# An attention and feed-forward kernel: the copy of each finished PV quad out of PSUM moves from VectorE to ScalarE, and the order of work is laid out again for all engines

## What is computed

```python
x = x + layernorm(attention(layernorm(x)))
x = x + layernorm(ffn(layernorm(x)))

# attention: 16 heads of 16 features
q = x @ Wq;  latent = (x @ Wk + x @ Wv) @ W_down_kv
k = latent @ W_up_k;  v = latent @ W_up_v
scores = (q_h @ k_h.T) / 16 * decay[i, j]        # decay = exp(-0.0001 * |i - j|)
out = softmax(scores) @ v_h;  return concat(out) @ Wo

# ffn
xh = x @ hadamard
xq = per-row 4-bit quantization of xh;  wq = ternary quantization of the weight
return xq @ wq.T
```

## Time and profile before

| | |
|---|---|
| median of 3 runs | 1435.21 us (1431.94 to 1436.89) |
| the profiled execution | 1435.05 us, span 1433.2 us, mean granted TensorE clock 0.983 |
| busy, share of the span: PE, DVE, ACT, POOL | 94%, 82%, 77%, 58% |
| ScalarE's exp of off-diagonal units (L909) | 768 instructions, 759.8 us |
| PV matmuls (L720) | 4096 in the page's count, 525.4 us |
| VectorE's copy out of heads_ps (L1150) | 128 instructions, 87.2 us |

### The profile page before, as it was taken

One profiled execution on the slowest core, in us unless ns is written; L12 is line 12 of the kernel. 1 busy time (PEld: TensorE's weight loads), 2 busy tenths in 40 slices (PEclk: granted clock), 3 DMA queues, 4 the chain that ended last, 5 costly groups with the idle time before them and its releaser, 6 DMA issues.

```text
span 1433.2 us, 35971 instructions
## 1 busy us (share of the span) xinstructions
PE 1349.5 (94%) x12330; PEld 600.5 (42%) x12330; DVE 1179.9 (82%) x2739; ACT 1098.2 (77%) x1125; POOL 834.7 (58%) x1238
## 2 busy tenths in 40 slices
PE   5889999999999999999999999999999999999863
PEld 3334444444444444444444444444444444443332
DVE  7567888888888888888888888888888888888655
ACT  1878787888888788878878887887888787787831
POOL 4223655666565666556557655656765655675446
PEclk9999999999999999999999999999999999999986
DMA  6455456556555645656564565655556555555420
GB/s 194 154 167 170 154 172 202 155 164 206 164 182 173 197 156 166 206 157 190 173 190 157 173 201 157 193 175 187 156 177 194 163 185 184 176 156 175 128 77 31
DMA packets 174557, 241.45 MB, mean 168 GB/s; under 512 B 28336, under 2 KB 145200, under 8 KB 174512
## 3 DMA queue, kind: packets, MB, share of 16 engines
q1 hardware_dynamic: 140176, 206.78, 46.5%
q10 hardware_dynamic: 34336, 34.08, 7.7%
HBM read 154.80 MB, written 69.21 MB: 156 GB/s over the span
## 4 chain that ended last, share of the span: by engine, by line
PE 76%; DVE 8%; issue 5%; ACT 4%; DMA 3%; SPq 2%; POOL 2%; DVEq 0%; ACTq 0%; POOLq 0%
PE heads_ps L720 27%; PE scores_ps L707 16%; PE misc_ps L603 8%; PE misc_ps L635 7%; PE misc_ps L660 4%; PE misc_ps L614 3%; PE misc_ps L587 3%; ACT probs L909 2%; DVE x_hl L1204 2%; PE misc_ps L595 2%; PE misc_ps L678 2%; DVE diagonal L1253 2%; DVE weighted L1161 2%; PE misc_ps L625 2%; PE misc_ps L669 1%
## 5 line engine op out<-in xcount | busy, mean ns | idle before, releaser
L909 ACT ACTIVATE probs<-scores_ps 128x1024 f32<-128x1024 f32 x768 | 759.8, 1026 | 248.0 <-PE scores_ps L707 247.9
L720 PE MATMUL heads_ps<-probs,v_sb 128*32 128x512 f32 x4096 | 525.4, 603 | 3.6 <-DVE heads L1150 1.9
L1253 DVE TENSOR_TENSOR diagonal<-scores_ps,comp 128x1024 f32<-128x1024 f32 x256 | 312.2, 1219 | 70.1 <-PE scores_ps L707 70.1
L707 PE MATMUL scores_ps<-q_rep,k_rep 64*128 64x128 f16 (+2 forms) x5120 | 324.6, 251 | 16.0 <-DVE diagonal L1253 9.2
L707 PEld LDWEIGHTS scores_ps<-q_rep,k_rep 64*128 64x128 f16 x5120 | 165.6, 94 | 348.7 <-DVE diagonal L1253 149.5
L916 ACT ACTIVATE probs<-diagonal 128x2048 f32<-128x2048 f32 x128 | 246.0, 1922 | 0.0
L996 POOL TENSOR_TENSOR ln_neg_mean<-zero,ln_moments 128x4 f32<-128x4 f32 (+1 forms) x131 | 34.6, 264 | 356.5 <-DVE ln_moments L1115 356.3
L1161 DVE SCALAR_TENSOR_TENSOR weighted<-misc_ps,edges 128x384 f32<-128x384 f32 x256 | 129.4, 547 | 64.3 <-PE misc_ps L603 33.8
L720 PEld LDWEIGHTS heads_ps<-probs,v_sb 128*32 128x32 f32 x4096 | 91.5, 108 | 171.7 <-issue 169.8
L1038 POOL TENSOR_TENSOR q_hl<-weighted,q_hl 128x768 f16<-128x768 f32 x64 | 105.5, 1648 | 77.5 <-DVE q_hl L1168 77.5
L1043 POOL TENSOR_TENSOR heads_c<-heads_c,den_spread 128x1024 f32<-128x1024 f32 (+1 forms) x33 | 75.7, 2296 | 111.0 <-DMA den_spread<-den_scratch 111.0
(11 more groups left out here) (132 smaller groups left out, 1511.5 us busy)
## 6 DMA issues: line engine op xcount, KB each, us to landing
q_rep<-q_scratch SPq DMA_DIRECT2D x128, 384.0 KB, 4.3
k_rep<-k_scratch SPq DMA_DIRECT2D x256, 192.0 KB, 3.9
q_scratch<-q_hl SPq DMA_DIRECT2D x64, 384.0 KB, 2.6
k_scratch<-k_hl SPq DMA_DIRECT2D x64, 384.0 KB, 3.1
x_in<-in_L_attn_x_dram ACTq DMA_DIRECT2D x32, 512.0 KB, 4.9
heads_c<-heads SPq DMA_DIRECT2D x256, 64.0 KB, 2.5
...
den_spread<-den_scratch SPq DMA_DIRECT2D x256, 64.0 KB, 2.3
```

Of the source, the lines that this page charges most:

```text
L707: ins = mm(scores_ps[:, place + par, at:at + n * P], k_rep[rows, pair, kv_, k_cols], q_rep[rows, pair, qv_, q_cols], start=True, stop=True)
L720: ins = mm(heads_ps[W32 * g:W32 * (g + 1), :], v_sb[:, b.slot, kt, at:at + W32], probs[:, quad % 2, g, kt, :], start=(kt == 0), stop=(kt = ...
L909: nc.scalar.activation(flat[:, :, at:at + S], scores_ps[:, place:place + 2, :], ACT.Exp, scale=EXP_SCALE).then_inc(off_probs, 1)
L1253: v.tensor_tensor(diagonal[:, quad % 2, 2 * two:2 * two + 2, :], scores_ps[:, place:place + 2, :], comp[:].rearrange("p t n -> p (t n)").u ...
```

## The change

The copy of heads_ps becomes an ACTIVATE Copy on ScalarE, with the same waits and the same semaphore; its VectorE instruction is gone. All step lists and closing lists are replaced.

```diff
 TENSOR_STEPS = {
-    1: [("z", 0, 0), ("z", 1, 0), ("pv_end", 3, 0)], 3: [("xT", 0, 0), ("pv_end", 3, 1)], 5: [("xT", 1, 0), ("pv_end", 3, 2)],
-    7: [("pv_end", 3, 3), ("lat", 0, 0)], 9: [("q", 0, 0), ("q", 0, 1)], 11: [("pv", 0, 0), ("x1T", 0, 0)],
-    13: [("x1T", 1, 0), ("pv", 0, 1)], 15: [("k", 0, 0), ("pv", 0, 2), ("k", 1, 0), ("pv", 0, 3)], 17: [("v", 0, 0), ("xh", 0, 0)],
-    19: [("xh", 1, 0), ("pv", 1, 0)], 21: [("pv", 1, 1), ("pv", 1, 2)], 23: [("q", 1, 0), ("q", 1, 1), ("pv", 1, 3)],
-    25: [("y", 0, 0), ("y", 0, 1)], 27: [("pv", 2, 0), ("qintT", 0, 0)], 29: [("y", 1, 0), ("y", 1, 1)],
-    31: [("pv", 2, 1), ("pv", 2, 2), ("pv", 2, 3)],
+    0: [("z", 0, 0), ("z", 1, 0)], 1: [("xT", 0, 0)], 2: [("pv_end", 3, 0), ("pv_end", 3, 1)], 4: [("pv_end", 3, 2)], 5: [("xT", 1, 0)],
+    7: [("pv_end", 3, 3), ("lat", 0, 0)], 9: [("q", 0, 0), ("q", 0, 1)], 11: [("pv", 0, 0)], 12: [("x1T", 0, 0), ("x1T", 1, 0)],
+    13: [("pv", 0, 1)], 14: [("k", 0, 0)], 15: [("pv", 0, 2), ("k", 1, 0), ("pv", 0, 3)], 17: [("v", 0, 0), ("xh", 0, 0)],
+    19: [("xh", 1, 0), ("pv", 1, 0)], 21: [("pv", 1, 1), ("pv", 1, 2), ("pv", 1, 3)], 22: [("q", 1, 0)],
+    24: [("y", 0, 0), ("y", 0, 1), ("q", 1, 1)], 26: [("pv", 2, 0), ("pv", 2, 1), ("qintT", 0, 0)], 28: [("y", 1, 0), ("y", 1, 1)],
+    30: [("pv", 2, 2), ("pv", 2, 3)],
 }
 SCALAR_STEPS = {
-    4: [("load_res", 0)], 12: [("x1T", 0)], 14: [("x1T", 1)], 15: [("load_x", 0)], 21: [("round_x", 0)],
-    22: [("round_x", 1), ("round_x", 2), ("round_x", 3)], 30: [("qintT", 0)],
+    4: [("load_res", 0)], 10: [("heads_end", 3)], 12: [("x1T", 0), ("x1T", 1)], 13: [("load_x", 0)], 17: [("heads", 0)],
+    21: [("round_x", 0)], 22: [("round_x", 1), ("round_x", 2), ("round_x", 3), ("heads", 1)], 27: [("qintT", 0)], 31: [("heads", 2)],
 }
 VECTOR_STEPS = {
-    1: [("z", 0), ("z", 1), ("x1_make",)], 2: [("xT", 0)], 5: [("x1_stats",), ("xT", 1), ("x1_moments",), ("z_stats",)],
-    8: [("heads_end", 3)], 10: [("lat", 0), ("q_split", 0), ("z_moments",)],
-    15: [("x1_low", 0), ("x1_low", 1), ("k_split", 0), ("den_invert",), ("k_split", 1)], 17: [("v", 0)],
-    18: [("heads", 0), ("act_scales",)], 20: [("v", 1), ("x_stats",), ("x_moments",), ("q_split", 1)], 25: [("heads", 1)],
-    26: [("quantize",)], 27: [("y", 0)], 28: [("y", 1), ("y_stats",), ("y_moments",), ("heads", 2)],
+    0: [("x1_make",)], 1: [("x1_stats",)], 2: [("z", 0), ("xT", 0)],
+    4: [("z", 1), ("xT", 1), ("x1_moments",), ("z_stats",), ("lat", 0), ("z_moments",)], 11: [("q_split", 0)], 13: [("x1_low", 0)],
+    14: [("x1_low", 1), ("k_split", 0), ("den_invert",), ("k_split", 1)], 16: [("v", 0), ("act_scales",)],
+    21: [("v", 1), ("quantize",)], 24: [("y", 0), ("q_split", 1), ("x_stats",)], 26: [("x_moments",)],
+    30: [("y", 1), ("y_stats",), ("y_moments",)],
 }
-POOL_STEPS = ["x1_apply", ("q", 0), "rstd4", "add_out", ("k", 0), "heads_normalize", ("k", 1), "x_apply", ("q", 1), "rstd2"]
+POOL_STEPS = ["x1_apply", ("q", 0), "rstd4", "add_out", ("k", 0), "heads_normalize", ("k", 1), ("q", 1), "x_apply", "rstd2"]
-SYNC_STEPS = [("own", "spread", 1), ("a", "gather_den"), ("a", "pack_den"), ("pre", "store_q", 0), ("a", "compact", 1),
-              ("a", "return_den"), ("a", "spread_den"), ("pre", "store_k", 0), ("pre", "spread", 0), ("own", "compact", 0),
-              ("pre", "store_q", 1), ("pre", "store_k", 1), ("c", "store_out")]
+SYNC_STEPS = [("own", "spread", 1), ("a", "gather_den"), ("a", "pack_den"), ("a", "compact", 1), ("a", "return_den"),
+              ("pre", "store_q", 0), ("a", "spread_den"), ("pre", "store_k", 0), ("c", "store_out"), ("pre", "spread", 0),
+              ("pre", "store_q", 1), ("own", "compact", 0), ("pre", "store_k", 1)]
```

Of the closing lists, the places that are spoken of below:

```diff
 TENSOR_CLOSING = [
...
-    ("z", 3, None, 1, 0), ("x1T", 2, None, 0, 0), ("x1T", 2, None, 1, 0), ("xh", 2, None, 0, 0), ("xh", 2, None, 1, 0),
-    ("y", 1, 0, 0, 0), ("y", 1, 0, 0, 1), ("y", 1, 1, 1, 0), ("y", 1, 1, 1, 1), ("qintT", 2, None, 0, 0), ("z", 2, None, 0, 0),
+    ("z", 3, None, 1, 0), ("x1T", 2, None, 0, 0), ("x1T", 2, None, 1, 0), ("xh", 2, None, 0, 0), ("y", 1, 0, 0, 0),
+    ("xh", 2, None, 1, 0), ("qintT", 2, None, 0, 0), ("y", 1, 0, 0, 1), ("y", 1, 1, 1, 0), ("y", 1, 1, 1, 1), ("z", 2, None, 0, 0),
...
 VECTOR_CLOSING = [
-    ("z", 3, None, 0), ("heads_end", 1, None, 3), ("x1_make", 2, None), ("z", 3, None, 1), ("x1_stats", 2, None),
-    ("x1_moments", 2, None), ("z_stats", 3, None), ("den_invert", 1, None), ("z_moments", 3, None), ("x1_low", 2, None, 0),
+    ("x1_make", 2, None), ("z", 3, None, 0), ("den_invert", 1, None), ("x1_stats", 2, None), ("x1_moments", 2, None), ("z", 3, None, 1),
...
 POOL_CLOSING = [
-    ("x1_apply", 2, None), ("rstd4", 3, None), ("add_out", 3, None), ("heads_normalize", 1, 0), ("heads_normalize", 1, 1),
+    ("x1_apply", 2, None), ("heads_normalize", 1, 0), ("rstd4", 3, None), ("add_out", 3, None), ("heads_normalize", 1, 1),
...
 SYNC_CLOSING = [
-    ("gather_den", 1, None), ("pack_den", 1, None), ("return_den", 1, None), ("compact", 1, None, 1), ("spread_den", 1, None),
+    ("gather_den", 1, None), ("compact", 1, None, 1), ("pack_den", 1, None), ("return_den", 1, None), ("spread_den", 1, None),
```

The copy itself:

```diff
+            def heads_take(b, hq):
+                act.wait_ge(pv_done, count(SLOTS, b, T * (hq + 1)))
+                if hq == 0 and not (isinstance(b.number, int) and b.number == 0):
+                    act.wait_ge(den_gathered, count(64, b, 0))
+                    act.wait_ge(heads_compacted, count(128, b, 0))
+                nc.scalar.activation(heads[:, hq, :], heads_ps[:], ACT.Copy).then_inc(heads_taken, 1)
...
-            def heads_take(b, hq):
-                dve.wait_ge(pv_done, count(SLOTS, b, T * (hq + 1)))
-                if hq == 0 and not (isinstance(b.number, int) and b.number == 0):
-                    dve.wait_ge(den_gathered, count(64, b, 0))
-                    dve.wait_ge(heads_compacted, count(128, b, 0))
-                v.tensor_copy(heads[:, hq, :], heads_ps[:]).then_inc(heads_taken, 1)
```

More of the change, by code:

```diff
@@ L115 @@
-    ("x1_low", 2, None, 1), ("act_scales", 2, None), ("quantize", 2, None), ("y", 1, None, 0), ("y_stats", 1, 0), ("y_moments", 1, 0),
-    ("y", 1, None, 1), ("y_stats", 1, 1), ("x1_make", 1, 0), ("y_moments", 1, 1), ("z", 2, None, 0), ("x1_stats", 1, 0),
-    ("x1_moments", 1, 0), ("z", 2, None, 1), ("x1_make", 1, 1), ("x1_stats", 1, 1), ("x1_moments", 1, 1), ("z_stats", 2, None),
-    ("z_moments", 2, None), ("x1_low", 1, 0, 0), ("x1_low", 1, 1, 1), ("act_scales", 1, 0), ("act_scales", 1, 1), ("quantize", 1, 0),
@@ L1241, in _ @@
                      "q_split": lambda b, part: weigh(b, "q", part), "k_split": lambda b, part: weigh(b, "k", part),
-                     "heads": heads_take, "heads_end": heads_take, "den_invert": den_invert,
+                     "den_invert": den_invert,
                      "y_stats": y_stats, "y_moments": y_moments, "x1_make": x1_make, "x1_stats": x1_stats, "x1_moments": x1_moments, "z": z_take,
```

19 lines of the change are left out of this document (12 added, 7 removed), and 2 rows, old and new, of the table TENSOR_CLOSING.

## The result

The changed kernel takes **1460.36 us** (median, 1458.50 to 1461.43), the kernel before 1435.13 beside it: a ratio of 1.0177, 95% interval 1.0156 to 1.0198, slower by 1.8%. The forecast was 1463.

The account below looks back on a forecast made before the run. TensorE bounds the kernel, busy 197.3 of 200 us. -0.88 + 0.1 + 0.77 + 0.65 = +0.64 us an iteration, +18 over 28, plus 2 and 8, gives +28 on 1435.05: 1463 us, range 1446 to 1480.

Parts of the forecast that it names:

- the early and late iterations: Iterations outside the 28 full ones: the same seam with less TensorE work to cover it, +2 us in all.
- The waits at k: TensorE's waits around both k stages for VectorE's x1_low and k_split vanish: -0.88 us an iteration, bounds 0 and -0.88.
- The copy at the seam: Between iterations, pv_end waits for signal, heads 2 copy, exp and diag_exp (3.6 us) against 2.85 of TensorE work: +0.77 an iteration.
- Scores that chase their exp: Score units at S(7) and S(24) wait for late exps on ScalarE: +0.65 us an iteration, bounds 0 and 0.9.
- TensorE's order: Same TensorE work cut differently: more score stretches (+0.40), more joined PV pieces (-0.26): sum +0.1 us an iteration.
- VectorE, SyncE, GpSimd at nothing in the loop: Moved work on these three engines in the steady iteration ends nothing last: each booked at 0.
- The collision rival: VectorE's k cast meets GpSimd's add of out_sb every iteration, TensorE waits 1.46 us: +69 us, 1504; chance 0.06.
- After the last iteration: Closing lists: second y part 7.4 us later, x1 of batch 2 4.0 later, lying beside each other: +8 us, bounds 0 and 12.
- Faster: Rival: ScalarE's added waits don't show on TensorE; -0.78 an iteration, +8 at the end, 1421 us; chance 0.17.
- No change: Rival: only the seam is real, loop sums to 0, end 0 to 8: 1435 to 1443 us; chance 0.15.

Follow-up runs that it names:

- after: The changed kernel itself, with the whole change, measured against the kernel before: 1460.36 us, ratio 1.0177.
- k_alone: The kernel before with only the k part: x1T joined at step 12, x1_low at steps 13 and 14, first k at step 14: 1415.65 us, 0.9869.
- four_pieces: The changed kernel with heads 2 alone copied on ScalarE in four pieces of 128 columns: 1467.05 us, ratio 1.0234.
- copy_on_vector: The changed kernel's lists with the four copies of heads_ps back on VectorE: 1452.86 us, ratio 1.0127.
- seam: The changed kernel with PV piece (2,3) back at step 31 and heads 2 on ScalarE behind diag_exp: 1461.67 us, ratio 1.0152.
- before_scalar: The kernel before, its lists kept, with the four copies of heads_ps on ScalarE, heads 2 behind diag_exp: 1503.5 us, ratio 1.0486.
- best_pool: seam plus pv_end's last piece one step earlier, the closing lists of the kernel before, and GpSimd's first k split ahead of add_out: 1455.04 us.
- k_scalar: k_alone with the four copies on ScalarE (steps 10, 18, 25, behind diag_exp at 31) and SyncE's compact ahead of store_q: 1434.34 us, 0.9983.

## Why the prediction was right, and where not

The forecast of 1463 against 1460.4 holds by its main steps, and partly by luck, because two errors cancel: the loop with the early and late iterations came out 7 us cheaper (12.5 measured, 20 booked) and the end 6 us dearer (13.9 measured, 8 booked).

*The waits at k* (-0.88 booked). In after the first k, the PV behind it and the second k take 0.51 + 1.01 + 0.63 = 2.15 us, with no wait 0.52 + 0.99 + 0.52 = 2.03; so 0.12 are left, and the gain is -0.76. k_alone bears it out, with a median iteration of 41.27 in place of 41.90 and some 19 us less in all, -0.6 an iteration for the k part with its cuts.

*The copy at the seam* (+0.77; 3.6 - 2.85 would be 0.75). Measured +0.81, with 3.57 us for the 3.6. Right in mechanism and size; four_pieces moves it one for one. But the copy is the smaller part of it: copy_on_vector, with pv_end as early, is only 0.19 us shorter from z to pv_end. And seam shows that it is not what undoing it gives back: 0.50 came free there, and 0.37 of it went into cuts and into the scores ahead of v.

*Scores that chase their exp* (+0.65). This term was too large. Step 7 starts 0.60 behind step 6 in place of 0.32: +0.28, booked +0.3. At step 24 it is 0.65 for the two units of steps 23 and 24 in place of 0.54, so +0.1 where I had 0.2 to 0.35. I had wrongly let that unit lose its join with step 23.

*TensorE's order* (+0.1, bounds -0.3 and +0.4). What is left of +0.36 after these terms: 0.36 + 0.76 - 0.81 - 0.38 = -0.07, within the bounds.

*VectorE, SyncE, GpSimd at nothing in the loop*. True for after, and by luck. Its second cast of k starts between 0.2 and 1.1 us ahead of the add from one iteration to the next, which my walk had put at 0.5. The collision rival (0.06) was right in mechanism and place. Its price is a coincidence: the 1504 hold 0.64 us an iteration and 10 us at the end that only the lists of after have, and 1.46 for a meeting; before_scalar has neither of the former and comes to 1503.5 because an iteration with the meeting, the late exp and, in 16 of them, the second meeting costs 2.5 us. What I had not seen is that the kernel before stands 0.2 us from it, and that any change of the lists can decide on which side a kernel falls.

*After the last iteration* (+8, bounds 0 and 12; "These lie beside each other"). This is the step that failed. It measured +10.7 for the closing, inside its bounds, and 3.2 more at the last PV, which I had not listed: the seam with nothing behind it, and 1.6 of the 3.2 because the clock fell there. The two terms don't lie beside each other; with den_invert's place and TensorE's order put back, the closing fell by 3.1, and with the rest by 7.7 more.

*Rivals.* Faster fell with the seam, whose four terms need 3.57 against 2.76. No change needed a loop at nothing and an end of at most 8; they cost 12.5 and 13.9.

What beats both kernels is the one part of the change for which the profile of before had shown a wait of TensorE. For the rest no run shows a gain: no regular wait of TensorE in before hung on the copy (1.9 us in the whole run), VectorE had 28 of 200 us free, and in the four pairs of runs that differ by the copy's engine the kernel with the copies on VectorE is the faster one (after, before_scalar, best_pool, k_scalar; in the last, SyncE's order differs too).
